# A recommender tower on one core: VectorE's last pair product one slot later, GpSimd's low parts in another order

## The reference

```python
def cin(x0, filters):                     # x0 = e, (512, 32, 32)
    prev, outs = x0, []
    for W in filters:                     # (1, 32*32, 128), (1, 32*128, 128)
        z = einsum('bhd,bmd->bhmd', x0, prev).reshape(b, h * m, d)
        prev = relu(einsum('bpd,pn->bnd', z, W[0]))
        outs.append(prev)
    return concatenate(outs, axis=1).sum(axis=-1)
h = concatenate([cin(e, (filter_0, filter_1)), dense_ctx], axis=1)
h = relu(h @ W_top1 + b_top1); h = relu(h @ W_top2 + b_top2); y = h @ W_top3
```

## Time and profile before

| | |
|---|---|
| runs | 908.58 us median of 3 (907.87 to 910.68) |
| profiled execution | 908.48 us, span 906.7 us |
| busy share of the span | PE 93%, DVE 82%, ACT 80%, POOL 79% |
| granted TensorE clock, mean | 0.996 of full |
| transfers | 124.41 MB, 137 GB/s mean |

### The profile page before, as it was taken

One profiled execution on the slowest core, in us unless ns is written; L12 is line 12 of the kernel. 1 busy time (PEld: TensorE's weight loads), 2 busy tenths in 40 slices (PEclk: granted clock), 3 DMA queues, 4 the chain that ended last, 5 costly groups with the idle time before them and its releaser, 6 DMA issues.

```text
span 906.7 us, 18108 instructions
## 1 busy us (share of the span) xinstructions
PE 846.9 (93%) x3607; PEld 668.3 (74%) x3607; DVE 748.0 (82%) x2363; ACT 726.2 (80%) x2418; POOL 716.1 (79%) x739
## 2 busy tenths in 40 slices
PE   0189999999998999999999999999999999999997
PEld 0167777777786777787777777787777777787873
DVE  4158888898886889888888898888888998888893
ACT  2158888988886898988888888888888898888882
POOL 7777899878887889878888989877777766677761
PEclk9999999999999999999999999999999999999999
DMA  7035676666765666666577565766676665655440
GB/s 191 12 91 134 156 171 150 145 141 136 158 146 142 147 146 149 136 150 146 144 166 165 141 155 114 156 145 142 161 166 144 143 147 127 155 139 144 94 93 1
DMA packets 59774, 124.41 MB, mean 137 GB/s; under 512 B 9377, under 2 KB 18145, under 8 KB 59746
## 3 DMA queue, kind: packets, MB, share of 16 engines
q0 software_dynamic: 22240, 68.17, 40.2%
q1 hardware_dynamic: 37506, 55.96, 19.7%
HBM read 54.99 MB, written 3.05 MB: 64 GB/s over the span
## 4 chain that ended last, share of the span: by engine, by line
PE 60%; DVE 13%; POOL 12%; issue 11%; DMA 1%; ACT 1%; DVEq 1%; SPq 0%; POOLq 0%; ACTq 0%
PE bank L871 49%; DVE acc L765 10%; PE bank L809 9%; POOL rows L344 4%; POOL pair_low L382 2%; POOL half L364 2%; POOL rows_next L397 1%; POOL parts L356 1%; DVE pair L629 1%; PE bank L918 1%; POOL w_sb L366 1%; DVE parts L765 1%; DVE cur_low L640 1%; DMA shifts<-x_scratch 1%; ACT parts L563 0%
## 5 line engine op out<-in xcount | busy, mean ns | idle before, releaser
L563 ACT ACTIVATE parts<-bank,x 128x128 f32<-128x128 f32 x2048 | 591.6, 382 | 118.0 <-PE bank L871 108.6
L765 DVE SCALAR_TENSOR_TENSOR acc<-bank,x,acc 128x128 f32<-128x128 f32 x1792 | 485.3, 342 | 94.2 <-PE bank L871 94.1
L871 PE MATMUL bank<-w_high,cur_high 128*128 128x512 f32 x1024 | 407.5, 398 | 5.7 <-DVE acc L765 3.6
L871 PE MATMUL bank<-w_low,cur_high 128*128 128x512 f32 x1024 | 400.1, 391 | 0.0
L871 PE MATMUL bank<-w_high,cur_low 128*128 128x512 f32 x992 | 388.6, 392 | 0.0
L871 PEld LDWEIGHTS bank<-w_high,cur_high 128*128 128x128 f32 x1024 | 192.5, 188 | 62.3 <-DVE acc L765 19.1
L871 PEld LDWEIGHTS bank<-w_low,cur_high 128*128 128x128 f32 x1024 | 192.6, 188 | 39.4
L871 PEld LDWEIGHTS bank<-w_high,cur_low 128*128 128x128 f32 x992 | 186.5, 188 | 41.2
L364 POOL TENSOR_TENSOR half<-parts 128x512 f32<-128x512 f32 x126 | 165.1, 1310 | 61.5 <-DMA parts<-parts 61.3
L382 POOL TENSOR_TENSOR pair_low<-pair,pair_high 128x512 fp32r<-128x512 f32 x124 | 158.6, 1300 | 28.0 <-ACT pair_high L498 24.0
L397 POOL DMA_INDIRECT rows_next<-table_dram,ids_next x96 | 98.1, 1022 | 30.6 <-issue 30.3
(11 more groups left out here) (90 smaller groups left out, 492.1 us busy)
## 6 DMA issues: line engine op xcount, KB each, us to landing
parts<-parts POOLq DMA_DIRECT2D x126, 512.0 KB, 5.7
shifts<-x_scratch SPq DMA_DIRECT2D x155, 256.0 KB, 3.9
x<-x_scratch SPq DMA_DIRECT2D x31, 256.0 KB, 2.9
x_scratch<-turned SPq DMA_DIRECT2D x31, 64.0 KB
rows_next<-table_dram,ids_next POOLq DMA_INDIRECT x96
wt<-w_top_dram SPq DMA_DIRECT2D x2, 512.0 KB
x_scratch<-turned SPq DMA_DIRECT2D x31, 32.0 KB
rows<-table_dram,ids_sb POOLq DMA_INDIRECT x32, 2.4
```

What stands on the lines that cost most here:

```text
L563: ins = nc.scalar.activation(parts[q][ab][:, at:at + N2], act_bank[ab][:, i * N2:(i + 1) * N2], ACT.Copy, scale=x0[u][:, h, 2 * q + ab:2 * ...
L765: nc.vector.scalar_tensor_tensor(out=dst, in0=dve_bank[e % 2 * 2 + ab][:, i * N2:(i + 1) * N2], scalar=x0[u][:, h, 2 * q + ab:2 * q + ab + ...
L871: return nc.tensor.matmul(dst[:], cur_half[u][:, cols], w1_half[:, fields], **flags)
```

## The change

DVE makes step 4's product before the group at slot 16, no longer before the one at slot 12, and ACT rounds it after slot 17, no longer after slot 16. In POOL's pass with t % 4 == 0 the low part of step 4 now stands behind `add_halves`, and that of step 3 alone before it. In the pass with t % 4 == 2 the low parts of steps 1 and 2 stand before the gathers, no longer behind them. PE's order does not change, and no instruction is added or taken away but register and loop code.

```diff
-DVE_PAIR = {0: (1,), 4: (2, 0), 8: (3,), 12: (4,)}
+DVE_PAIR = {0: (1,), 4: (2, 0), 8: (3,), 16: (4,)}
 PAIR_ORDER = [step for steps in DVE_PAIR.values() for step in steps]
-ACT_PAIR_HIGH = {4: 1, 8: 2, 13: 3, 16: 4}
+ACT_PAIR_HIGH = {4: 1, 8: 2, 13: 3, 17: 4}
...
                     if t % DC == 0 and (next_block or t < tiles - DC):
-                        pair_lows(k * CPB + t // DC + 1, (2, 3))
+                        pair_lows(k * CPB + t // DC + 1, (2,))
                     add_halves(k * (tiles // 2) + t // 2, t // 2 % 2)
+                    if t % DC == 0 and (next_block or t < tiles - DC):
+                        pair_lows(k * CPB + t // DC + 1, (3,))
+                    if t % DC == 2 and (next_block or t < tiles - DC - 2):
+                        pair_lows(k * CPB + t // DC + 2, (0, 1))
                     for s in (t, t + 1):
                         if (next_block and s < rows_at) or (one_after and s > rows_at):
                             for f in late[s]:
                                 gather(f)
-                    if t % DC == 2 and (next_block or t < tiles - DC - 2):
-                        pair_lows(k * CPB + t // DC + 2, (0, 1))
```

## The result

| | median us | runs | ratio to before (95% interval) |
|---|---|---|---|
| before | 908.58 | 5 (907.87 to 910.68) | |
| changed | 949.36 | 5 (947.67 to 951.5) | 1.045 (1.043 to 1.0471) |

The change costs 40.8 us; the forecast was 954.5 us, 46 more than before. The profiled execution took 951.22 us, span 949.4, mean clock 0.993.

What follows compares the result with a forecast made beforehand. PE, busy 93%, was taken as the bound. 19 chunks x 2.3 = 43.7, plus 2.65 and 1 for chunk 8, minus 1.7 already paid, plus 0.5, gave 46.2 more than 908.5: forecast 954.5 us, range 942 to 972.

Steps and rivals of the forecast that it cites:

- What bounds the kernel: PE, busy 93% of the span, sets the time; only its idle time counts, with 4.2 us of waits for POOL.
- slack of 0.38 at step 3: In chunk 9 POOL finishes step 3's low part at 311.49 and PE begins with it at 311.87.
- the signs that I had named: PE's waits for POOL: 20 to 40, 40 to 50 us, chunks 1 to 20 only; POOL's waits for ACT's rounding: about 42.
- The half with the transfers moved forward: Passes with t % 4 == 0: POOL's gain ends at its wait for DVE's MACs; zero for PE, bounds minus 4.2 us and zero.
- The half with the gathers moved back: Passes with t % 4 == 2: gathers no longer cover POOL's wait for ACT's rounding; 2.3 us per chunk, chunks 1 to 20.
- the worked chunk: Chunk 9 traced through POOL: step 3's low part 2.0 us late for PE, step 4's 2.2 us late in all.
- Chunk 8: POOL's 3.44 us stop behind the loop's jump stays, and new lateness comes on top in full: 2.65 us, plus 1 for clock.
- The term of 1 for the clock: A longer stretch at the lower clock in chunk 8 adds 1 us, from 0 to 1.7.
- Chunk 18: PE's existing wait of 1.30 is already paid; POOL's stop of 1.92 before a gather may show, taken as 0.5 us.
- Rival A: PE's clock falls in many of the new stops, 1.5 us more each: 970 for ten chunks, 984 for all; chance 0.20.
- Rival B: Gathers cost less behind the low parts, their gaps falling into the wait for ACT: 0.6 us per chunk, 942; chance 0.09.
- Rivals C and D: C: POOL reaches step 2 after ACT has rounded it, 902.6. D: PE makes up its lateness, 908.5. Chance 0.03 each.

Runs made afterwards that it cites:

- e2: Kernel before with both tables changed and step 4's low part behind `add_halves`, gathers left where they were: 908.48 us, ratio 0.9998.
- e1: Kernel before with only the low parts of steps 1 and 2 put before the gathers (t % 4 == 2): 945.48 us, ratio 1.0398.
- e4: Changed kernel with all gathers in the passes with t % 4 == 0, none at t % 4 == 2: 914.85 us, ratio 1.0059.
- e11: Changed kernel with step 3's low part before `sum_left`: 946.74 us, ratio 1.042.
- e3: Kernel before with DVE's and ACT's tables alone changed, POOL's order as before: 909.24 us, ratio 0.9997.
- e5: Changed kernel with the two gathers between the low parts of steps 1 and 2: 917.43 us, ratio 1.0083.
- e12: e1 with step 3's low part before `sum_left`: 921.16 us, ratio 1.0133.
- e6: Kernel before with POOL's loop over blocks 0 and 1 written out: 906.09 us, ratio 0.9966.
- e9: Kernel before with step 3's low part before `sum_left`: 906.05 us, ratio 0.9966.
- e10: Kernel before with step 3's low part before `sum_left` and POOL's loop written out: 903.67 us, ratio 0.9935.

## Why the prediction was right

**What bounds the kernel.** Right. PE's idle time was the time to look at: chunks 1 to 20 grew by 40.5 us, and the median by 40.8. The slack of 0.38 at step 3 was the number that mattered. Of the signs that I had named, PE has 20 waits for POOL, but of 35.1 us and not 40 to 50: an idle time of 1.65 makes step 3 start 1.8 late, and what the restart and step 4 add is not in that sum. POOL's waits for ACT's rounding went to 61 and not to 42, because it now waits 0.70 before step 1 as well; that costs nothing, since step 2 has a later wait behind it.

**The half with the transfers moved forward, at zero.** Right for this half alone: e2 gives 908.48 against 909.18, no difference clear of noise. It also went as said. POOL gains 25.7 us of its waits for transfers (61.3 to 35.6) and gives the same 25.7 back at DVE's MACs (20.8 to 46.5).

**The half with the gathers moved back.** Right, and most terms of the worked chunk came out within hundredths. In chunk time the worked example put step 2's start where it came; the interval from step 2's end to the first sum was to be 2.69 and is 322.83 - 320.32 = 2.51; from there to step 3's low part 5.53, and is 328.36 - 322.83 = 5.53; step 3's low part to step 4's end 3.22, and is 332.90 - 329.63 = 3.27. PE's delay came out at 2.2 and not 2.3 per chunk. The term mis-sized is the gap before the first gather: 0.12 to 0.16 behind a low part, 0.30 behind the transfer issues. The forecast had 5.7 us more than the 40.5 by which chunks 1 to 20 grew; the 18 of them other than 8 and 18 make 2.6 of that. ACT's side went about as worked out too. It was 1.1 late at slot 17 in the text; its waits for `half` are 40 of at most 0.9, 34.3 us in all, and no wait of PE within the chunks is put down to ACT's `parts`.

**Chunk 8.** The step "this stays, and the new lateness comes on top in full" is the one that failed. I had 3.65 (2.65 of lateness and 1 of clock) and it is 1.4. Timeline of POOL there, against the earlier trace rows:

```profile
298.40 1.26 POOL L382 TENSOR_TENSOR pair_low<-pair,pair_high 128x512 fp32r<-128x512 f32 x1 [1.47 <-issue]
```

The stop behind the jump shrank from 3.44 to 1.47 us, and so took up 2.0 of the 2.5 us by which POOL reached the jump later. PE idled 3.24 and not 2.76, which is 0.5 more and not 2.65. The term of 1 for the clock held: the clock was low for 6.8 us (before 3.4), of which the first 1.3 fell into PE's idle time, so 5.5 us of work ran at half rate, 1.0 us more lost than before.

**Chunk 18.** I had 2.3 - 1.3 and 0.5 for POOL's stop before a gather, should it show; it was 0.7. There is no such stop of POOL in chunk 18 any more, and chunk 18 had already been 1.55 longer than an even chunk before, not 1.3. This is 0.8 of the 5.7, and chunk 8 the remaining 2.3.

**Rival A, the clock.** Wrong for this kernel. The profiled execution has twenty stops for low parts, 19 with an idle time of 1.57 to 1.75 and that of chunk 8 with 3.24, and only at this one was the clock at 1.2 GHz. Windows of 1 us in chunk 8 (length; PE, PEld, DVE, ACT, POOL busy; clock; DMA share, GB/s):

```profile
298.00:299.00 1.00, 0.00 (x0) 0.00 (x0) 0.00 (x0) 0.05 (x1) 0.60 (x1) 0.70 0.03 8
299.00:300.00 1.00, 0.29 (x1) 0.29 (x2) 0.00 (x0) 0.00 (x0) 1.00 (x3) 0.50 0.00 0
...
304.00:305.00 1.00, 1.00 (x4) 0.71 (x3) 0.53 (x3) 0.01 (x1) 0.70 (x2) 0.50 1.15 225
305.00:306.00 1.00, 1.00 (x5) 0.87 (x4) 1.00 (x5) 0.45 (x2) 0.76 (x1) 0.88 1.10 205
```

The stops of e1 cost none either outside chunk 8. The idle times of PE in chunk 8 of the other runs do not sort by length alone: 1.94 (e2) and 2.19 (e4) left the clock at 1.00, while 2.17 (e11) was followed by 3.4 us at 1.2 GHz, as were 2.60 (e3), 2.76 (before), 3.39 (e5) and 3.51 (e1). In the setup it fell behind 1.89 (before, e11) and 1.93 (e12), but not behind 2.21 (e3), 2.37 (changed), 2.49 (e1) and 2.63 (e6). The Trainium skill, "TensorE: Matmul & The Clock Gate", section "Why this matters for your kernels", asks for no idle gaps above about 3 us. For the 19 stops of about 1.65 it was the better guide, but the clock fell after 2.76 and 2.17, so here its limit is too high.

**Rival B** was a part of the truth: of the 0.6 per chunk it supposed, 0.15 to 0.2 came. **Rivals C and D** did not occur; POOL ended its issues at 315.48 and ACT had step 2 rounded at 318.95, the 3.5 us that spoke against C.

## What to carry to other kernels

Before moving work out of an in-order queue's wait, ask what it was hiding: two gathers that looked like a delay for two low parts cost nothing in front of them, because the second low part could hardly have started before they were over, and they cost about 2 us of every chunk behind it. Then follow the queue to the next result that somebody waits for, and to the one after it: e11 shows that taking away the first stop gives next to nothing (3 of 41 us) if the next result ends the same chain. And a wait that an engine off the critical path loses is not a gain until its next wait is looked at: e2 moved 26 us of POOL's idle time from one place to another and the time stayed the same within noise.

## What the runs showed of the hardware that I had not expected

**The stop behind POOL's jump is not of a fixed length.** With the same loop but other code in it, POOL idled behind the jump for very different times, and tends to idle less when it gets there later in chunk time:

| POOL reaches the jump at | idle behind it |
|---|---|
| 14.5 to 14.7 | 3.44 (before), 3.27 (e3), 3.00 (e4), 2.61 (e2) |
| 15.3 | 3.44 (e5) |
| 15.7 | 2.08, and 1.38 a little later (e9) |
| 17.1 | 1.74 (e1), 1.47 (changed) |
| 18.2 | 1.13 and 1.33 (e12), 0.40 and 0.40 (e11) |

The first two lines show that the time of arrival is not all of it. With the loop written out the stop in chunk 8 was gone (e6, e10), and one of 1.24 came up in chunk 9. The Trainium skill, "Runtime: NRT & Kernel Launch", section "Instruction fetch mechanics", has the taken branch force a fetch, and e6 agrees; that the place of the code in its pages sets the rest wasn't tried and stays open.

**The clock around an idle time of PE near the end differs from run to run.** Before a transpose at the end PE idles 2.73 to 2.75 us in each of the twelve profiled executions. In that of the kernel before the clock stayed at 1.00 afterwards. In the other eleven it fell to 1.2 GHz within 2.4 us of that idle time's end, for 3.4 us in nine and for 6.8 us in two (the changed kernel and e10). These windows are of the changed kernel:

```profile
933.00:934.00 1.00, 0.15 (x1) 0.15 (x1) 0.33 (x2) 0.00 (x0) 0.00 (x0) 0.64 0.00 0
934.00:935.00 1.00, 0.64 (x2) 0.35 (x3) 0.00 (x0) 0.27 (x1) 0.00 (x0) 0.50 0.02 8
```

The stretch from the start of chunk 31 to the end took 46.3 us without the fall, 47.4 to 48.1 with 3.4 us of it and 48.7 and 48.9 with 6.8, which accounts for the 2.4 us above. The five runs of the changed kernel lie between 947.67 and 951.5, and mean clocks between 0.998 and 0.993 go with them, the lower clock with the longer time. What decides between these cases, at the same idle time, stays open.
